# A four-layer decoder kernel: last gated stage's units in pairs on different rows, closing-stage preparation moved into the layers, new orders of work

## The reference

```
log_D = where(tril, cs[t] - cs[s] + igate[s], -inf)     # cs: cumulative sum of log sigmoid of a gate
D = exp(log_D - max_log_D)
C = (q @ k.T / sqrt(DH)) * D                            # per head: 128 x 128
h = (C / (max(|sum C|, exp(-max_log_D)) + 1e-6)) @ v
h = layernorm of each head * weight
```

```
w_scale = mean(|weight|);  q_weight = sign(weight) * (|weight| > 0.5 * w_scale)
i_scale = max(|x|) / 127   # over all eight samples
q_input = clip(round(x / i_scale), -128, 127)
out = q_input @ q_weight.T * w_scale * i_scale + bias
x = layernorm(x + out)
```

## Time and profile before

| what | value |
| --- | --- |
| median of 3 runs | 1097.37 us (1094.23 to 1098.67) |
| the profiled execution's own time | 1096.83 us |
| its span, first to last instruction | 1095.0 us |
| busy, share of the span | PE 87%, PEld 64%, DVE 52%, ACT 42%, POOL 4% |
| mean granted TensorE clock | 0.917 of full |
| DMA | 33 GB/s mean |

### The profile page before, as it was taken

The page is one execution under the profiler, slowest core; times in us unless marked ns, Lnnn a source line. Parts: engine busy times, 40 slices in busy tenths (PEclk is TensorE's granted clock), DMA queues, the critical chain, the costliest instruction groups (busy, mean ns, idle before and its releaser), DMA issues. The chain is left out here.

```text
span 1095.0 us, 20449 instructions
## 1 busy us (share of the span) xinstructions
PE 951.1 (87%) x8329; PEld 695.7 (64%) x8329; DVE 569.7 (52%) x1585; ACT 455.9 (42%) x905; POOL 45.2 (4%) x68
## 2 busy tenths in 40 slices
PE   6588989899999979978797989999989998988691
PEld 4246858688787956564256657778777785664341
DVE  5833566643555663356516655665256565354216
ACT  2136533463466734532233433234456672541211
POOL 0300000100100000000000000000010000000000
PEclk9999989999899999789779999999999998986855
DMA  9100000310003011030000000300000300000000
GB/s 324 34 1 2 1 1 21 136 35 1 18 1 131 1 40 40 10 130 1 1 11 1 1 2 2 121 35 34 1 18 1 131 1 1 1 1 1 2 0 19
DMA packets 6830, 35.97 MB, mean 33 GB/s; under 512 B 722, under 2 KB 4306, under 8 KB 5459
## 3 DMA queue, kind: packets, MB, share of 16 engines
q1 hardware_dynamic: 6738, 34.68, 8.6%
HBM read 34.15 MB, written 0.52 MB: 32 GB/s over the span
## 5 line engine op out<-in xcount | busy, mean ns | idle before, releaser
L644 PE MATMUL bank<-xT,weights_F 128*128 128x256 f32 x832 | 207.1, 392 | 0.4
L644 PEld LDWEIGHTS bank<-xT,weights_F 128*128 128x128 f32 x832 | 153.8, 195 | 28.8 <-issue 8.9
L652 PEld LDWEIGHTS bank<-weights_F,p 128*128 128x128 f32 x1088 | 136.5, 195 | 14.7 <-issue 6.6
L652 PE MATMUL bank<-weights_F,p 128*128 128x128 f32 x1088 | 142.4, 280 | 2.0 <-DVE p L1325 2.0
L1697 ACT ACTIVATE p<-bank 128x512 f32<-128x512 f32 x160 | 84.6, 604 | 121.9 <-PE bank L490 106.5
L1309 DVE SCALAR_TENSOR_TENSOR res<-bank,comb,res 128x128 f32<-128x128 f32 x184 | 55.5, 344 | 66.7 <-PE bank L652 65.1
L1150 DVE TENSOR_REDUCE m_wide<-bank 128x4 f32<-128x512 f32 x96 | 60.0, 683 | 34.4 <-PE bank L751 25.7
L1325 DVE TENSOR_TENSOR p<-p,bank 128x512 f32<-128x512 f32 x72 | 49.2, 684 | 53.5 <-ACT p L1769 33.2
L1769 ACT ACTIVATE p<-bank 128x512 f32<-128x512 f32 x72 | 42.7, 597 | 74.1 <-PE bank L644 73.7
L1641 ACT ACT_TABLE_LOAD x42 | 53.9, 1283 | 14.3 <-PE bank L516 7.0
L1845 ACT ACTIVATE p<-bank 128x512 f32<-128x512 f32 x64 | 37.2, 599 | 54.5 <-PE bank L644 54.3
(11 more groups left out here) (323 smaller groups left out, 1476.1 us busy)
## 6 DMA issues: line engine op xcount, KB each, us to landing
weights_F<-in_L1f SPq DMA_DIRECT2D x2, 4096.0 KB, 13.3
weights_F<-in_L0f SPq DMA_DIRECT2D x2, 3456.0 KB, 13.1
weights_F<-in_L2f SPq DMA_DIRECT2D x2, 3456.0 KB, 11.7
weights_Y<-in_L1x_kv SPq DMA_DIRECT2D x2, 1024.0 KB, 10.8
weights_Z<-in_L1x SPq DMA_DIRECT2D x2, 1024.0 KB, 11.8
weights_Y<-in_L2a SPq DMA_DIRECT2D x2, 898.0 KB, 4.5
weights_Z<-in_L2x SPq DMA_DIRECT2D x2, 449.0 KB, 3.4
weights_L3m<-in_L3m SPq DMA_DIRECT2D x2, 288.0 KB, 7.1
```

What stands on the lines that cost most here:

```text
L644: m = mm(b[:, k * NT:(k + 1) * NT], W[weight][:, f:f + P], s.xT[:], start=True, stop=True)
L652: m = mm(b[:, tk(u)], h[:, tk(u)], w, start=k == 0, stop=k == len(chunks) - 1)
```

## The change

It has four parts.

1. L3x on TensorE: `unit(i)` becomes `units(first, second)`, called for (0, 3) and then (1, 2). The four banks of the ring are opened two at a time, the products of the two units are issued next to one another, and the last product reads 32 partitions in place of 8. `retrieved(0)` and `retrieved(1)` follow. ACT and DVE follow in the order 0, 3, 1, 2.
2. The closing stage's preparation moves into the layers. After each L3x DVE takes the largest |x| of the pair's new x (into one column of `amax` per pair). In stream b's first turn, about L1x, DVE sums |weight|, TensorE adds that over partitions (one extra step), and DVE makes thresholds and ternary weights (four extra steps). GpSimd adds the bias while it copies x to `x_all`.
3. The closing stage itself: the maximum over partitions is one product that yields it on every partition, and one reduction; the quantising is two passes of DVE in halves and one of ACT that subtracts the rounding constant, with the products of a half following it; the eight normalisations are split between DVE and ACT.
4. New strings in `TURN_ORDER` for all five engines. Two more constants (`ones_bf`, `zeros_bf`) are made at the start and waited for; `warm`, which could issue extra products, is given empty lists and issues none.

The diff, cut:

```diff
 TURN_ORDER = {
     "pe":
...
-        "b3 a2 b1 a1 b1 a1 b2 a2 b2 a1 b1 a1 b2 a1 b1 a2 b2 a2 b3 a1 b1 a3 b5 a1 b1 a2 b1 a3 b2 a4 b5 a1 b1 a1 b2 "
...
-        "a3 b1 a2 b1 a1 b1 a4 b2 a1 b20 ",
...
+        "a1 b2 a3 b1 a1 b2 a1 b3 a1 b1 a1 b2 a2 b2 a2 b3 a4 b2 a4 b1 a2 b1 a1 b1 a1 b2 a9 b3 a2 b2 a2 b6 a1 b15 "
+        "a1 b3 a1 b1 a1 b2 a1 b1 a1 b1 a1 b3 a2 b2 a1 b1 a3 b3 a2 b2 a1 b1 a1 b1 a3 b3 a1 b1 ",
...
-        "a2 b6 a1 b2 a8 b1 a2 b6 a1 b4 a1 b4 a1 b2 a3 b9 a2 b2 a2 b2 a2 b4 a1 b1 a2 b4 a1 b2 a4 b20 ",
...
+        "b4 a2 b2 a4 b5 a5 b2 a6 b2 a2 b9 a6 b2 a1 b2 a6 b2 a1 b5 a1 b6 a1 b2 a12 b2 a2 b4 a3 b1 a1 b6 a1 b13 a1 "
+        "b2 a3 b2 a2 b11 a2 b2 a1 b1 a3 b3 a1 b2 a3 b2 a2 b2 a1 b1 a2 b2 a1 b1 a2 b2 a1 b2 a1 ",
...
-                    def unit(i):
-                        u, half = i // 2, i % 2
-                        b = opened("dve", "L3x", "s", i)
-                        mm(heads(b[:], 4), s.ctxT[rows64(half), tk(u)], s.bd_c[rows64(half), u], start=True, stop=True) \
-                            .then_inc(ring.filled((pair, "L3x", "s", i)), 1)
-                        b = opened("act", "L3x", "D", i)
-                        mm(heads(b[:], 4), ident_bf[:], among(neg_causal_t_bf[:], 4), start=True, stop=False)
-                        filled(mm(heads(b[:], 4), const("ones")[32 * u:32 * u + 8, 0:T],
-                                  s.m_diag8[32 * u:32 * u + 8, 4 * half:4 * half + 4], start=False, stop=True), "L3x", "D", i)
+                    def units(first, second):
+
+                        both = (first, second)
+                        banks = [opened("dve", "L3x", "s", i) for i in both]
+                        for i, b in zip(both, banks):
+                            u, half = i // 2, i % 2
+                            filled(mm(heads(b[:], 4), s.ctxT[rows64(half), tk(u)], s.bd_c[rows64(half), u], start=True, stop=True),
+                                   "L3x", "s", i)
+                        banks = [opened("act", "L3x", "D", i) for i in both]
+                        for b in banks:
+                            mm(heads(b[:], 4), ident_bf[:], among(neg_causal_t_bf[:], 4), start=True, stop=False)
+                        for i, b in zip(both, banks):
+                            u, half = i // 2, i % 2
+                            filled(mm(heads(b[:], 4), const("ones")[rows32(u), 0:T], s.m_diag8[rows32(u), 4 * half:4 * half + 4],
+                                      start=False, stop=True), "L3x", "D", i)
...
-                    unit(0)
-                    yield
-                    unit(1)
+                    units(0, 3)
+                    yield
+                    units(1, 2)
                     yield
...
                     retrieved(0)
                     yield
-                    unit(2)
-                    yield
-                    unit(3)
-                    yield
                     retrieved(1)
...
+                        if pair == 1 and stage is L1x:
+                            pe.wait_ge(*told("w_partial"))
+                            filled(mm(opened("dve", "w_sum")[:, 0:1], const("ones")[:, 0:P], w_stat[:, 0:1], start=True, stop=True), "w_sum")
+                            yield
...
-            pe.wait_ge(S("masks"), 3)
+            pe.wait_ge(S("masks"), 5)
...
+                    dve.wait_ge(*done[-1])
+                    o.count(dve.tensor_reduce(amax[:, pair:pair + 1], s.x_tok[:].rearrange("p u d -> p (u d)"), X, ALU.max,
+                                              apply_absolute_value=True), S("amax_partial"))
...
+                def ternary_weights():
+                    link(dve.tensor_scalar(w_stat[:, 1:2], bank("w_sum")[:, 0:1], 1.0 / (D * D), None, ALU.mult), free("w_sum"))
+                    for k, half in enumerate((0.5, -0.5)):
+                        done = o.count(dve.tensor_scalar(w_stat[:, 2 + k:3 + k], w_stat[:, 1:2], half, None, ALU.mult))
...
+                        done = o.count(dve.tensor_scalar(wq[:, k], W["L3f_w"][:], w_stat[:, 2 + k:3 + k], None, compare))
...
+                    o.count(dve.tensor_tensor(w_bf[:], wq[:, 0], wq[:, 1], ALU.subtract), S("w_ternary"))
...
-                    yield from rest(lambda: o.count(pool.tensor_copy(x_all[:, pair * NS:(pair + 1) * NS], s.x_tok[:]), sem("kept")))
+                    yield from rest(lambda: o.count(pool.tensor_tensor(x_all[:, pair * NS:(pair + 1) * NS], s.x_tok[:],
+                                                                among(W["L3f_b"][:], NS), ALU.add), sem("kept")))
...
+            pe.matmul(psum[0][:, 0:P], amax[:, 4:5].to_broadcast([P, P]), IDENT, start=True, stop=True).then_inc(fin["turned"], 1)
...
+            o.count(dve.tensor_reduce(amax[:, 4:5], amax[:, 0:4], X, ALU.max), fin["partial"])
             dve.wait_ge(fin["turned"], 1)
+            link(dve.tensor_reduce(amax[:, 5:6], psum[0][:, 0:P], X, ALU.max), st)
+            link(dve.tensor_scalar(amax[:, 6:7], amax[:, 5:6], 1.0 / 127.0, None, ALU.mult), st)
+            link(dve.reciprocal(amax[:, 7:8], amax[:, 6:7]), st)
             for g in range(2):
+                link(dve.tensor_scalar(q_in[:, cols(g)], xT_all[:, cols(g)], amax[:, 7:8], ROUND, ALU.mult, ALU.add), st)
+                o.count(dve.tensor_scalar(q_in[:, cols(g)], q_in[:, cols(g)], ROUND - 128.0, ROUND + 127.0, ALU.max, ALU.min),
+                        fin["rounded"])
...
+                act.wait_ge(fin["rounded"], g + 1)
+                act.activation(q_bf[:, cols(g)], q_in[:, cols(g)], ACT.Identity, bias=const("eps")[:, 4:5]).then_inc(fin["operands"], 1)
...
+            for g in range(2):
+                dve.wait_ge(fin["rstd"], g + 1)
+                own = slice(g * HALF, (g + 1) * HALF)
+                o.count(dve.scalar_tensor_tensor(shift8[:, own], mv8[:, own, 0], -1.0, rstd8[:, own], ALU.mult, ALU.mult), fin["shift"])
+                for b in samples(g)[2:]:
+                    o.count(dve.tensor_scalar(y_all[:, b, :], x_all[:, b, :], mv8[:, b, 0:1], rstd8[:, b:b + 1],
+                                              ALU.subtract, ALU.mult), fin["normed_dve"])
...
+                for b in samples(g)[:2]:
+                    act.activation(y_all[:, b, :], x_all[:, b, :], ACT.Identity, scale=rstd8[:, b:b + 1], bias=shift8[:, b:b + 1]) \
+                        .then_inc(fin["normed_act"], 1)
```

More of the change, by code:

```diff
@@ L412, in _, with warm @@
             mm, tr = pe.matmul, pe.transpose
+            def warm(b, n):
+                for _ in range(n):
+                    mm(heads(b[:], 4), ident_bf[:], among(zeros_bf[:], 4), start=True, stop=True)
             def program(g):
@@ L416, in program @@
                 key = pair = turn = None
+                warmth = iter(WARM["ab"[g]].split())
                 def opened(by, *a):
-                    return ring.open((pair, *a), by)
+                    b = ring.open((pair, *a), by)
+                    warm(b, int(next(warmth, 0)))
+                    return b
                 def filled(ins, *a):
@@ L1567, in keep @@
                         return o.count(dve.tensor_copy(held[u][:, 0:HC * 17], b[:, 0:HC * 17]), free("L3x", "o", u))
-                    unit(0)
-                    yield
-                    unit(1)
-                    yield
+                    for i in (0, 3, 1):
+                        unit(i)
+                        yield
                     keep(0)
@@ L1622, in program @@
                     for stage in (L0a, L0x, L0f, L1a, L1x, L1f, L2a, L2x, L2f, L3a, L3x):
+                        if pair == 1 and stage is L1x:
+                            yield from sum_weights()
                         yield from stage()
+                        if pair == 1 and stage is L1x:
+                            yield from ternary_weights()
             for s in streams:
@@ L1935, in L3x @@
                     yield
-                    for i in range(4):
+                    for i in (0, 3, 1, 2):
                         exp_ln()
@@ L2135, in program @@
                         if turn + 1 < TURNS and st == "L3x":
-                            sp.wait_ge(*ring.full((pair, "L3x", "s", 3)))
+                            sp.wait_ge(*ring.full((pair, "L3x", "s", 2)))
                             sp.wait_ge(S(f"L3x_v17_{g}"), turn + 1)
@@ L2179, in _build, with cols, samples @@
     rstd8 = sb("rstd8", [P, B])
+    shift8 = sb("shift8", [P, B])
     fin = {n: ctx.enter_context(nc.semaphore(f"ffn_{n}")) for n in
-           ("partial", "turned", "whole", "spread", "operands", "products", "var", "rstd", "normed")}
+           ("partial", "turned", "rounded", "operands", "products", "var", "rstd", "shift", "normed_dve", "normed_act")}
     fin_step = ctx.enter_context(nc.semaphore("ffn_dve_step"))
     fin_act = ctx.enter_context(nc.semaphore("ffn_act_step"))
+    stored = ctx.enter_context(nc.semaphore("stored"))
     ROUND = float(1.5 * 2 ** 23)
-    stored = ctx.enter_context(nc.semaphore("stored"))
+    HALF = B // 2
+    WIDE = HALF * T
+    def cols(g):
```

(20 more changed lines are left out.)

99 lines of the change are left out of this document (50 added, 49 removed), and 48 rows, old and new, of the table TURN_ORDER.

## The result

| | before | changed |
| --- | --- | --- |
| median (lowest to highest) of 18 runs each, us | 1097.69 (1094.0 to 1102.59) | 1086.86 (1075.62 to 1098.0) |
| ratio of the times, 95% interval | | 0.987 [0.985, 0.990] |
| profiled execution, its own time / span, us | 1096.83 / 1095.0 | 1080.39 / 1078.4 |

So the change saves 11 us by the medians and 14 by the ratio, where 23 were forecast. The ratio leaves out the runs over 1.5% above the fastest of their kernel, five of the changed kernel's and none of the other's, although they are only the upper end of one continuous spread; the medians of all runs give 0.990. The single times of the changed kernel spread over 22 us, and go with the mean granted clock of TensorE in each: 1075.62 at 0.935, 1096.67 at 0.914, some 10 us for each 0.01.

The account below looks back on a forecast made before the run. The kernel was taken as bound by TensorE where the two streams fill each other's gaps, by latency elsewhere. 1096.83 - 19.5 (orders) - 4.8 (closing stage) + 1.3 (preparation) = 1073.8, so 1074 us; range 1048 to 1091.

Parts of the forecast that it names:

- The sum: Profiled execution's own time: 1096.83 - 19.5 - 4.8 + 1.3 = 1073.8; median 0.5 us above, so 1074.
- rival B: The new orders bring nothing, since gains at the end were spent earlier: 1088.5 us, chance 0.17.
- Part 1: L3x units in pairs: 16.8 us less over four L3x if every wait is covered; 3.4 us in the last.
- The 32 rows in place of 8 cost nothing: L3x's log D product: reading 32 rows instead of 8 adds no time.
- rival A: Clock stays up: the two last L3x get 2.4 GHz and L2x's idle is filled; 1054 us, chance 0.27.
- The trace shows no drain: TensorE in L3x: changing tiling mode drains nothing; two products and the mask fill the 2.50 us.
- Parts 2 and 3: Preparation moved into the layers costs 1.3 us; the closing stage, now 14.5 us, saves 4.8 us.
- Part 4: New orders, the largest term: the layers end at 1058 against 1077.5, 19.5 us less.
- the second stream leaves L2f: Stream b's last exit from L2f: 970.3 becomes 948.2, plus 9 us idle, 957; near 955 would show it right.
- More idle before 900 than now: Sign of being wrong: more TensorE idle before 900 us, which would make rival B or Rival C of it.
- The other half of part 4: After 957: L3a of both streams 49 us plus 3 for b's turn-around, both L3x 49, ending at 1058.
- Rival C: Slower: stretches in lock step starve TensorE as both streams wait at once; 1105 us at 0.50, chance 0.11.

Follow-up runs that it names:

- ln_one_by_one: Changed kernel with before's orders up to b's second L1a, but each L3x unit's three products issued together: 1111.3 us, ratio 1.012 to before.
- old_orders: Changed kernel with the order strings of the kernel before throughout, fitted to the pairs and moved steps: 1075.5 us, ratio 0.980 to before.
- no_pairs: Kernel before's strings and L3x units, with only the changed kernel's moved preparation and new closing stage: 1095.9 us, ratio 0.997 to before.
- mid_first: Changed kernel with before's orders up to b's second L1a, except changed orders from 210 to 385 us: 1078.3 us, ratio 0.985 to before.
- late_new_2: Second timing of the changed kernel with before's orders up to b's second L1a: 1066.3 us, ratio 0.973 to before.
- mid_second: Changed kernel with before's orders up to b's second L1a, except changed orders from 385 to 740 us: 1066.8 us, ratio 0.973 to before.

## Why the prediction was right, and where not

**The sum.** The time falls in the stated range and on the forecast side, 13 us above the forecast of 1074. It is outside the forecast's own range (1063 to 1084) and only 1.6 us from rival B's 1088.5. Half of the 13 us is in the profiled execution, whose own time is 6.6 us above the sum of 1073.8; the median of the runs lies another 6.5 above it, where the step from profiled execution to median was put at 0.5. For the kernel before that held; the changed one has a wider spread of clocks.

**Part 1** was right in its terms: 1.13 us a pair, 16.8 us of work for the four L3x (16.5 by ln_one_by_one), waits of 3.14 and 2.15 for a stream alone. "The 32 rows in place of 8 cost nothing" is true, but they bring 7 to 8 us by the clock, and the pairs bring clock wherever L3x runs (some 19 us in old_orders). That was rival A's mechanism, which I had tied to the two last L3x side by side only. There it was granted in part: 0.75 and 0.58 of the clock in L3x beside L3x. So rival B's price of the pairs, 5.4 us without the orders, was too low by some 14 (19 measured). "The trace shows no drain" says too much. Between other products one mask product takes 0.32 us start to start (995.40 to 995.72); two in a row take 0.26 each in the changed kernel (1033.98 to 1034.50), four in a row 0.24 (982.83 to 983.80). So a cost under 0.1 us at each change of rows is possible; for the sum it does not matter.

**Parts 2 and 3**: 3 us together, 3.5 forecast (no_pairs). The chain is 10.4 where 9.7 was forecast: the sum of a half starts 4.24 us after the first maximum and not 3.9, and the shifts and last normalisations take 1.5 (1073.80 to 1075.33) where 1.0 was put.

**Part 4 is the step that failed**, in its first half: "the second stream leaves L2f" at 957. TensorE's work there ended at 968.6, 11.6 later. The sum had 9 us of new idle for L2x beside L2a in the second turn, and nothing for the first turn, whose pairing of stages was held to change little. But there too the new strings put a's first L2x beside b's L2a. Adding idle and clock up to 960 us gives 139.6 us before and 160.4 after, so 20.8 were lost, not 9. "More idle before 900 than now", named as a sign of being wrong, did show (91.9 us before, 113.5 after). mid_first puts 11 to 13 of these in one stretch of 210 to 385 us. The 9 us for the second turn were nearly right: old_orders and late_new_2 run alike up to 697 us (landmarks within 0.2), and b leaves L2f at 964.4 in the one and 958.4 in the other, 6.0 earlier, where the steps of a that moved behind it were put at 12.4 + 1.35 = 13.75 us; so 7.8 were lost.

The other half of part 4 made good half of this error: the L3a pair took 45.5 us (968.6 to 1014.1), 52 forecast, the L3x pair 50.4 (to 1064.5), 49 forecast. Rival B's reason, that what the dense products had covered comes back as idle, is thus what happened, in the early part only; the late part gains 9 to 11 us. The orders as a whole, counted as the largest gain (14.5 us more than B), cost some 9. One bound of this part is added up wrongly: 58.8 us of work at 0.74 take 79.5 us from 957 on, which is -41 and not -36; nothing hangs on it. How the 22.8 us of work for the two L3x were got is not written down; 21.9 were measured.

**Rival C** would have needed under 0.52 of an engine in the lock-step stretches. L3a beside L3a did 37.53 x 0.99 = 37.2 us of work in 45.4, or 0.82; L3x beside L3x 13.4 + 8.5 = 21.9 of 50.6, or 0.43, but the forecast counted this stretch at 0.47 (22.8 in 49), so little was left for it to take. Together the two did 0.62.

That the total lies in the range, and so near rival B's number, is therefore in part luck, two errors that cancel: the pairs brought 19 us in place of 5.4 without the orders, and the orders took 9 in place of bringing 14.5.

**What the best version is**: the changed kernel with before's orders up to b's second L1a (late_new), 0.972 [0.967, 0.977] and again 0.973 [0.971, 0.976], 16 us below the changed one run beside it (1084.5 to 1068.1). mid_second equals it (0.973).

## What to carry to other kernels

An order of work written out by hand is judged stretch by stretch: for each, which latency-bound stage now stands beside which, and where the dense products went that filled it. If a repeated part of the schedule gets a new pairing, its price is to be counted in each repetition. Products on few rows were worth putting beside each other here for the clock as much as for their own time; count work, clock and idle apart, or the one hides the other.

## What of the hardware was not expected

- TensorE was busy almost without a gap (41.05 of 42 us) and was granted 1.2 GHz, with products on 64 and 32 rows one after another (ln_one_by_one); the same products with neighbours on different rows had 2.4 GHz after one or two pairs (changed, late_new, late_new_2). The difference was 23 to 30 us of clock in one kernel.
- Reading 32 partitions in place of 8 in one product, the added rows doing no work in the result, was worth 7 to 8 us by the ratios. The profiles show some 6 of clock for it, all after 1000 us, where the two last L3x stand side by side. What makes the clock come back earlier is not shown.
- One kernel's runs spread by 22 us with the granted clock (0.935 to 0.914). Even with the same strings, a left its first L0x at 94.3 us in old_orders' profile and 94.4 in late_new_2's, and at 100.5 in late_new's; the clock had cost 4.5 us by 120 us in the first and 9.4 in the last. What sets this is open.
